# Two attention layers on one core: how the softmax denominators travel, and the order of the last two units

## The chip, the core and the metric

The kernel runs on one core of a Trainium2 chip. Its engines work side by side, each through its own list of instructions, and wait for each other by semaphores: TensorE (PE, with its weight loads shown as PEld), VectorE (DVE), ScalarE (ACT), GpSimd (POOL), and SyncE (SP), which only issues transfers. The metric is the device time of one execution in microseconds; lower is better.

## What is computed

The input is x of shape (4, 64, 32, 32): four images, 64 channels, 1024 positions. Two layers follow each other. Each does, for every image:

```
h      = group_norm(x, 32 groups)             # 2 channels x 1024 positions in a group
q,k,v  = h Wq + bq, h Wk + bk, h Wv + bv      # 1x1 convolutions, 64 -> 64
scores = q k^T / sqrt(64)                     # 1024 x 1024
attn   = softmax(scores, over the keys)
x      = x + (attn v) Wo + bo
```

The layers differ in weights and in the epsilon of the norm (1e-5, 1e-6). The second layer works on the output of the first.

## The kernel before, in words

**Units.** A unit is one image in one layer. There are UNITS = 8, in the order of the images of layer 0, then of layer 1; LAST = 7. Unit u reads `xs` slot u and writes slot u + 4. Channels lie on partitions, twice: partitions 0 to 63 hold positions 0 to 511, partitions 64 to 127 hold 512 to 1023.

**Inside a unit.** The scores are built transposed, keys on partitions, queries along the row, in eight tiles t of 128 keys by 1024 queries. ScalarE takes the exponential of each tile into `probs[t]` (L448). `values` (L843 to 853) multiplies each with `vals` and sums into `ps_attn`. The query's maximum is subtracted as an extra row `q_row` in the scores (L837, L838). It comes from a pass over partial scores made a unit ahead: `partial_max` on PE (L778, L779), eight reductions `part` on VectorE (L583), `join` (L606), a transpose `turn_max` on PE (L792), a copy `stage_max` on ScalarE (L436), and two transfers `place_rows` on SP (L246).

**The denominators.** The eight tiles of `probs` are added elementwise into `prob_sum`: `first_add` on VectorE adds tiles 0 and 1 (L613), then POOL adds tiles 2 to 7 (`add`, L322), each 128x1024. `denominators` on PE sums over the 128 partitions with eight matmuls of 128 columns against `parity`, a 0/1 pattern of two interleaved column sets; the result, 128x128, lies in `ps_misc`: quarter q of the partitions holds queries 256 q to 256 q + 255, even rows the first 128 and odd rows the second. `reciprocal` (L621) on VectorE makes `block_rden`, and eight transfers `spread_rden` bring it to `rden` (128x512), the layout of `attn`: six on SP (L256) and two on ScalarE's queue (L464); for unit 0 and unit 6 all eight on SP. `finish` on POOL (L328, L331) then multiplies `attn` by `rden` and adds x.

**Order.** In pass w of the main loop PE makes the scores of unit w and, between them, the maxima of unit w + 1; then `denominators(w - 1)`, `values(w, 0..5)`, `turn_max(w + 1)`, `project(w + 2)`, `values(w, 6)`, `project_v(w + 2)`, `values(w, 7)`. On VectorE a pass is: the eight parts with `first_add(w)` behind the third, `join`, the statistics of unit w + 2, `reciprocal(w - 1)`, then `affine`, `low_front` and `low_back` of unit w + 2. Between statistics and `affine` POOL takes the root of the variance (`root`, L303). On ScalarE: eight exps, `apply_norm(w + 2)` (L379), the two spreads, `stage_max(w + 1)`, then the copies of the projection. On SP: `place_rows(w + 1)`, the spreads of unit w - 1, four transfers that make `cross` for unit w + 2 (L229 to L238), and a store. On POOL: the adds of unit w, with `root(w + 2)` behind tile 4 and `finish(w - 1)` behind tile 5. Everything after `affine(w + 2)` on the way to `project(w + 2)` therefore waits for the root. An exp of unit w + 1 into `probs[t]` waits until tile t of unit w is added.

**The tail.** For unit 6 POOL adds only tiles 2 to 5; VectorE adds 6 and 7 to each other (`pair_tail`) and then to the sum (`add_tail`, L642). For unit 7 POOL adds tile 2 and VectorE tiles 3 to 6 (`add_late`, L651); tile 7 goes straight into the sums on PE (`denominators_last`). Units 5 and 6 are finished on VectorE (`finish_tail`, L657, L660). Unit 7's reciprocals are spread by PE (`spread_last`, L906), not by transfers.

## Time and profile before

| | us |
|---|---|
| median of three runs | 213.41 |
| lowest and highest | 212.4, 216.33 |
| the profiled execution, its own time | 212.74 |
| its span, first to last instruction | 210.9 |

| engine | busy us | share of the span | instructions |
|---|---|---|---|
| PE | 181.2 | 86% | 1295 |
| DVE | 134.3 | 64% | 200 |
| POOL | 126.0 | 60% | 79 |
| ACT | 103.1 | 49% | 137 |

The mean granted clock of TensorE was 0.95 of its full 2.4 GHz. All durations come from the profiled execution, so a sum made of them is to be set beside 212.74 or 210.9 first, and only then beside the median. Busy shares are averages over stages that have different limits; what an engine waits for is read from the timeline and the waits.

### The profile page before, as it was taken

The numbers are of one execution on the slowest core, as the hardware profiler recorded it, in microseconds if no ns is written. First come the engines' busy times: TensorE is split into PE (matmuls) and PEld (weight loads), VectorE is DVE, ScalarE is ACT, GpSimd is POOL, SyncE is SP. The second block draws the span as 40 slices with busy tenths as digits, with TensorE's granted clock in tenths as the row PEclk, the third lists the DMA queues.
The fourth block names the chain that finished last, engine by engine and source line by source line (L and its number), as shares of the span: only waits on it lengthen the run. The fifth ranks groups of instructions, "written<-read, shape, count | busy, mean of one in ns | idle before, by whom it ended". The sixth has DMA issues, their size and how long they took to land.

```text
span 210.9 us, 3456 instructions
## 1 busy us (share of the span) xinstructions
PE 181.2 (86%) x1295; PEld 100.2 (47%) x1295; DVE 134.3 (64%) x200; ACT 103.1 (49%) x137; POOL 126.0 (60%) x79
## 2 busy tenths in 40 slices
PE   7797999999997786998987994999949989995473
PEld 4444753674365421675245731576315653672332
DVE  3799894699387821499639870399605993065443
ACT  4485773684566405296077512576035850690001
POOL 3443198848508995299934999079970999603000
PEclk9999999999999996799999999699979999999679
DMA  6453000400014000320014100150001500110111
GB/s 166 144 112 79 0 0 5 100 2 3 1 48 102 5 0 13 82 55 3 0 26 99 29 0 6 34 115 2 0 16 39 149 3 12 32 56 0 40 63 50
DMA packets 8896, 8.90 MB, mean 42 GB/s; under 512 B 1656, under 2 KB 5936, under 8 KB 8880
## 3 DMA queue, kind: packets, MB, share of 16 engines
q1 hardware_dynamic: 7648, 7.90, 15.3%
q10 hardware_dynamic: 1232, 0.79, 1.3%
q8 instruction: 10, 0.16, 0.3%
q14 instruction: 6, 0.05, 0.1%
HBM read 1.58 MB, written 1.05 MB: 12 GB/s over the span
## 4 chain that ended last, share of the span: by engine, by line
POOL 41%; issue 22%; PE 15%; DVE 12%; SPq 4%; DMA 3%; POOLq 1%; ACT 0%; DVEq 0%; ACTq 0%
POOL prob_sum L322 34%; PE ps_both L853 6%; DVE part_max L583 5%; SPq L256 4%; POOL xs L331 3%; POOL attn L328 3%; DMA rden<-block_rden 2%; DMA xs<-x_dram 1%; POOLq L52 1%; DVE prob_sum L613 1%; PE ps_scores L821 1%; PE ps_max L778 1%; PE ps_scores L837 1%; DVE block_rden L621 1%; PE ps_scores L823 1%
## 5 line engine op out<-in xcount | busy, mean ns | idle before, releaser
L322 POOL TENSOR_TENSOR prob_sum<-prob_sum,probs 128x1024 f32<-128x1024 f32 x41 | 100.5, 2457 | 20.7 <-DVE prob_sum L613 17.6
L448 ACT ACTIVATE probs<-ps_scores 128x1024 f32<-128x1024 f32 x62 | 63.0, 1026 | 21.9 <-PE ps_scores L838 12.7
L853 PE MATMUL ps_both<-probs,vals 128*64 128x512 f32 x224 | 55.0, 625 | 0.0
L583 DVE TENSOR_REDUCE part_max<-ps_max 128x2 f32<-128x1024 f32 x32 | 39.1, 1221 | 11.4 <-PE ps_max L779 11.3
L853 PEld LDWEIGHTS ps_both<-probs,vals 128*64 128x64 f32 x224 | 15.1, 142 | 28.2 <-issue 26.7
L328 POOL TENSOR_TENSOR attn<-attn,rden 128x512 f32<-128x512 f32 x5 | 7.1, 1419 | 34.1 <-DMA rden<-block_rden 34.1
L583 DVE TENSOR_REDUCE part_max<-ps_both 128x2 f32<-128x1024 f32 x21 | 25.6, 1220 | 2.3 <-PE ps_both L779 2.3
L837 PE MATMUL ps_scores<-q_row,ones_r 64*128 64x512 f32 x62 | 24.5, 395 | 0.5 <-ACT q_row L430 0.5
L838 PE MATMUL ps_scores<-q_row,ones_r 64*128 64x512 f32 x62 | 24.5, 396 | 0.0
L379 ACT ACTIVATE h<-xs,shift,gain 128x512 f32<-128x512 f32 x7 | 5.7, 811 | 34.6 <-DVE shift L550 34.6
L757 PE MATMUL ps_scores<-h,layer 64*128 64x512 f32 x16 | 10.9, 764 | 10.1 <-ACT h L379 9.7
L566 DVE SCALAR_TENSOR_TENSOR front<-ps_scores,layer,front 128x512 fp32r<-128x512 f32 x6 | 4.5, 751 | 20.1 <-ACT front L390 20.1
L583 DVE TENSOR_REDUCE part_max<-ps_scores 128x2 f32<-128x1024 f32 x11 | 13.4, 1219 | 0.9 <-PE ps_scores L779 0.9
L613 DVE TENSOR_TENSOR prob_sum<-probs 128x1024 f32<-128x1024 f32 x8 | 13.4, 1670 | 0.0
L837 PEld LDWEIGHTS ps_scores<-q_row,ones_r 64*128 64x128 f32 x62 | 11.4, 184 | 3.4 <-issue 0.7
L821 PE MATMUL ps_scores<-front,back 64*128 64x512 f32 x31 | 12.9, 415 | 0.0
L822 PE MATMUL ps_scores<-back,cross 64*128 64x512 f32 x31 | 12.8, 415 | 0.0
L821 PE MATMUL ps_scores<-front,cross 64*128 64x512 f32 x31 | 12.3, 398 | 0.0
L822 PE MATMUL ps_scores<-back,front 64*128 64x512 f32 x31 | 12.3, 398 | 0.0
L826 PE MATMUL ps_scores<-back,cross 64*128 64x512 f32 x31 | 12.1, 391 | 0.0
L824 PE MATMUL ps_scores<-back,front 64*128 64x512 f32 x31 | 12.1, 391 | 0.0
L825 PE MATMUL ps_scores<-front,back 64*128 64x512 f32 x31 | 12.1, 391 | 0.0
(161 smaller groups left out, 411.5 us busy)
## 6 DMA issues: line engine op xcount, KB each, us to landing
cross<-front SPq DMA_DIRECT2D x16, 128.0 KB, 2.3
cross<-back SPq DMA_DIRECT2D x16, 128.0 KB, 2.3
rden<-block_rden SPq DMA_DIRECT2D x46, 32.0 KB, 1.9
xs<-x_dram SPq DMA_DIRECT2D x4, 256.0 KB, 4.4
out_dram<-xs SPq DMA_DIRECT2D x3, 256.0 KB, 2.0
rden<-block_rden ACTq DMA_DIRECT2D x10, 32.0 KB, 1.9
q_row<-max_rows SPq DMA_DIRECT2D x14, 2.0 KB
layer<-layers_dram SPq DMA_DIRECT2D x1, 194.5 KB, 2.7
```

The costliest lines, as they stand in the source:

```text
L322: pool.tensor_tensor(total[:, :], total[:, :], probs[t][:, :], ALU.add).then_inc(added, 1)
L328: pool.tensor_tensor(a[:, :], a[:, :], rden[:, :], ALU.mult).then_inc(normed, 1)
L448: act.activation(probs[t][:, :], scores_buffer(u, t)[:, :], ACT.Exp, scale=SCALE).then_inc(exp_done, 1)
L583: dve.tensor_reduce(part_max[u % 2][:, at:at + 2 * JS + 1:2 * JS], ps[:, :].rearrange("p (g n) -> p g n", g=2), AX.X, ALU.max, negate=True ...
L613: dve.tensor_tensor(prob_sum[u % 2][:, :], probs[0][:, :], probs[1][:, :], ALU.add).then_inc(first_added, 1)
L821: pe.matmul(left, key_top[top, hi], front_u[top, HI], start=True, stop=False)
L822: pe.matmul(right, key_low[low, hi], back_u[low, HI], start=True, stop=False)
L824: pe.matmul(right, key_low[low, hi], back_u[low, LO], start=False, stop=False)
L825: pe.matmul(left, key_top[top, lo], front_u[top, HI], start=False, stop=False)
L837: pe.matmul(left, ones_r[top, :], row[top, :], start=False, stop=True)
L838: pe.matmul(right, ones_r[low, :], row[low, :], start=False, stop=True).then_inc(scores_mm, 1)
L853: mm = pe.matmul(ps_attn[half * C:(half + 1) * C, :], v, probs[t][:, cols], start=(t == 0), stop=(t == TILES - 1))
```

## The change

- The denominators of units 0 to 6 are summed by four matmuls of 256 columns against ones, and so stand repeated on all 32 rows of a quarter. `reciprocal` for these units works on 128x256 (`quarter_rden`). Unit 7 keeps the old form.
- Spreading takes four transfers of 64 rows by 256 columns, all on SP, instead of eight of 64 rows by 128. The two on ScalarE's queue go. In passes 1 to 6 SP issues them ahead of `place_rows`.
- VectorE does `reciprocal(w - 1)` ahead of the statistics of unit w + 2 instead of behind them.
- POOL takes `root(w + 2)` behind tile 5 instead of 4, and `finish(w - 1)` behind tile 6 instead of 5.
- On PE `turn_max(w + 1)` stands behind `values(w, 4)`; `values(w, 5)` and `values(w, 6)` stand ahead of `project(w + 2)`, and the wait for `max_staged` is in every pass. In pass 6 `denominators(6)` follows `values(6, 7)`, ahead of the scores of unit 7.
- The tail: POOL adds nothing of unit 7, VectorE adds tiles 2 to 6. On VectorE the order becomes `pair_tail(6)`, `add_tail(6)`, `reciprocal(6)`, `finish_tail(5)`, `first_add(7)`, five late adds, `finish_tail(6)`, `reciprocal(7)`.

```diff
--- before.py
+++ after.py
...
     POOL_ADDS = TILES - 2
-    TAIL_ADDS = (4, 1)
+    TAIL_ADDS = (4, 0)
     HEAD_MAX = [0, 1, 2, JS, JS + 1, JS + 2, 3, JS + 3]
...
         block_rden = sb("block_rden", [P, P])
+        quarter_rden = sb("quarter_rden", [P, HALF // 2])
         rden = sb("rden", [P, HALF])
...
 
-        def rden_of(i):
-            rows = block_rden[QUARTER * (i // 2) + i % 2:QUARTER * (i // 2 + 1):2, :]
-            return rows.unsqueeze(1).broadcast_to([QUARTER // 2, 2 * C // QUARTER, P])
+        def rden_of(q):
+            return quarter_rden[quarter(q), :].unsqueeze(1).broadcast_to([QUARTER, C // QUARTER, HALF // 2])
 
...
                     sp.wait_ge(normed, u)
-                for i in range(TILES if u in (0, LAST - 1) else TILES - 2):
-                    n, j = divmod(i, JS)
-                    sp.dma_start(rden[n * C:(n + 1) * C, j * P:(j + 1) * P], rden_of(i)).then_inc(rden_in, 16)
+                for q in range(4):
+                    n, k = divmod(q, 2)
+                    sp.dma_start(rden[n * C:(n + 1) * C, k * HALF // 2:(k + 1) * HALF // 2], rden_of(q)).then_inc(rden_in, 16)
 
...
             for w in range(UNITS):
+                if 0 < w < LAST:
+                    spread_rden(w - 1)
                 if w + 1 < UNITS:
                     place_rows(w + 1)
-                if w:
+                if w == LAST:
                     spread_rden(w - 1)
...
                 a = attn[u % 2]
-                pool.wait_ge(rden_in, 128 * (u + 1))
+                pool.wait_ge(rden_in, 64 * (u + 1))
                 pool.wait_ge(attn_copied, u + 1)
...
                     add(w, t)
-                    if t == 4 and w + 2 < UNITS:
+                    if t == 5 and w + 2 < UNITS:
                         root(w + 2)
-                    if t == 5 and 0 < w < LAST - 1:
+                    if t == 6 and 0 < w < LAST - 1:
                         finish(w - 1)
...
                 act.activation(attn[u % 2][:, :], ps_attn[:, :], ACT.Copy).then_inc(attn_copied, 1)
-
-            def spread_rden(u):
-                act.wait_ge(rden_done, u + 1)
-                act.wait_ge(normed, u)
-                for i in range(TILES - 2, TILES):
-                    n, j = divmod(i, JS)
-                    act.dma_start(rden[n * C:(n + 1) * C, j * P:(j + 1) * P], rden_of(i)).then_inc(rden_in, 16)
 
...
                     apply_norm(w + 2)
-                if 1 < w < LAST:
-                    spread_rden(w - 1)
                 if w < LAST:
...
             def reciprocal(u):
-                sums = ps_misc[:, 0:P] if u < LAST - 1 else ps_max[:, HALF:HALF + P]
                 dve.wait_ge(den_mm, u + 1)
                 if u:
-                    dve.wait_ge(rden_in, 128 * u)
-                dve.reciprocal(block_rden[:, :], sums).then_inc(rden_done, 1)
+                    dve.wait_ge(rden_in, 64 * u)
+                if u < LAST:
+                    dve.reciprocal(quarter_rden[:, :], ps_misc[:, 0:HALF // 2]).then_inc(rden_done, 1)
+                else:
+                    dve.reciprocal(block_rden[:, :], ps_max[:, HALF:HALF + P]).then_inc(rden_done, 1)
 
...
                 dve.wait_ge(exp_done, TILES * LAST + t + 1)
-                if t == 3:
-                    dve.wait_ge(added, added_count(LAST, 2))
+                if t == 2:
+                    dve.wait_ge(first_added, UNITS)
                 else:
-                    dve.wait_ge(late_added, t - 3)
+                    dve.wait_ge(late_added, t - 2)
                 dve.tensor_tensor(total[:, :], total[:, :], probs[t][:, :], ALU.add).then_inc(late_added, 1)
...
                 a, n = attn[u % 2], u - LAST + 3
-                dve.wait_ge(rden_in, 128 * (u + 1))
+                dve.wait_ge(rden_in, 64 * (u + 1))
                 dve.wait_ge(attn_copied, u + 1)
...
                 join(w + 1, neg_max[:, :])
+                if w:
+                    reciprocal(w - 1)
                 if prep:
...
                     join_stats(w + 2)
-                if w:
-                    reciprocal(w - 1)
                 if prep:
...
             pair_tail(LAST - 1)
+            add_tail(LAST - 1)
+            reciprocal(LAST - 1)
             finish_tail(LAST - 2)
-            add_tail(LAST - 1)
             first_add(LAST)
-            add_late(3)
-            add_late(4)
-            reciprocal(LAST - 1)
-            add_late(5)
-            add_late(6)
+            for t in range(2, TILES - 1):
+                add_late(t)
             finish_tail(LAST - 1)
...
             def denominators(u):
-                if u == 0:
-                    pe.wait_ge(parity_set, 2)
                 if u == LAST - 1:
...
                     pe.wait_ge(added, POOL_ADDS * (u + 1))
-                if u == LAST - 1:
-                    pe.wait_ge(exp_done, TILES * LAST + 6)
-                    sums = ps_max[:, HALF:HALF + P]
-                else:
-                    sums = ps_misc[:, 0:P]
-                block_sums(sums, prob_sum[u % 2], True, True).then_inc(den_mm, 1)
+                for q in range(4):
+                    mm = pe.matmul(ps_misc[quarter(q), 0:HALF // 2], ones[:, 0:QUARTER],
+                                   prob_sum[u % 2][:, q * HALF // 2:(q + 1) * HALF // 2], start=True, stop=True)
+                mm.then_inc(den_mm, 1)
 
...
             def denominators_last():
-                pe.wait_ge(rden_done, LAST)
-                pe.wait_ge(late_added, TILES - 4)
+                pe.wait_ge(parity_set, 2)
+                pe.wait_ge(late_added, TILES - 3)
                 block_sums(ps_max[:, HALF:HALF + P], prob_sum[LAST % 2], True, False)
...
                 values(w, 4)
-                values(w, 5)
                 if w:
...
                 turn_max(w + 1)
+                values(w, 5)
+                values(w, 6)
                 if prep:
                     project(w + 2)
-                values(w, 6)
+                pe.wait_ge(max_staged, w + 2)
                 if prep:
-                    pe.wait_ge(max_staged, w + 2)
                     project_v(w + 2)
                 values(w, 7)
+                if w == LAST - 1:
+                    denominators(w)
 
...
                 scores(LAST, t)
-            pe.wait_ge(max_staged, UNITS)
+            pe.wait_ge(rden_done, LAST)
             values(LAST, 0)
             values(LAST, 1)
-            denominators(LAST - 1)
             values(LAST, 2)
...
```

## Rows read from the trace of the kernel before

**Rows 1.** The page, part 4: chain that ended last, shares of the span.

```profile
POOL 41%; issue 22%; PE 15%; DVE 12%; SPq 4%; DMA 3%; POOLq 1%; ACT 0%; DVEq 0%; ACTq 0%
```

**Rows 2.** Stages: from:to, length, busy (instructions) of each engine, PE clock, DMA share, GB/s.

```profile
39.63:59.43 19.80, 19.80 (x152) 10.73 (x151) 14.87 (x23) 12.36 (x15) 11.91 (x6) 1.00 0.10 23
59.43:88.00 28.57, 23.30 (x151) 12.47 (x149) 15.24 (x23) 12.25 (x15) 17.79 (x9) 0.88 0.15 36
...
161.31:180.44 19.13, 18.23 (x131) 9.63 (x129) 13.87 (x12) 9.07 (x10) 16.11 (x7) 1.00 0.21 52
180.44:210.90 30.46, 20.62 (x194) 13.52 (x192) 13.21 (x16) 8.67 (x10) 4.78 (x3) 0.88 0.14 42
```

**Rows 3.** Waits of POOL, whole span: instruction, releaser, total us, times, longest.

```profile
POOL attn L328 <- DMA rden<-block_rden: 34.1, 5, 8.1
```

**Rows 4.** Timeline of unit 3: start us, us, engine, line, operation, count, [idle before, releaser].

```profile
102.28 0.95 DVE L621 RECIPROCAL block_rden<-ps_both 128x128 f32<-128x128 f32 x1
...
104.19 0.55 POOL L303 TENSOR_TENSOR rstd<-var_eps,minus_half 128x1 f32<-128x1 f32 x1
...
105.20 0.81 ACT L379 ACTIVATE h<-xs,shift,gain 128x512 f32<-128x512 f32 x1 [5.71 <-DVE shift L550]
105.27 1.20 ACTq L464 DMA_DIRECT2D rden<-block_rden  x2
106.57 0.27 ACT L436 ACTIVATE max_rows<-ps_both 8x128 fp32r<-8x128 f32 x1 [0.55 <-issue]
...
106.86 1.35 SPq L246 DMA_DIRECT2D q_row<-max_rows  x2
108.31 3.81 SPq L256 DMA_DIRECT2D rden<-block_rden  x6
...
113.43 1.29 POOL L328 TENSOR_TENSOR attn<-attn,rden 128x512 f32<-128x512 f32 x1 [6.37 <-DMA rden<-block_rden]
```

**Rows 5.** Timeline of PE, unit 1 and the start of unit 2.

```profile
39.56 0.50 PE L778 MATMUL ps_max<-back,front 64*128 64x512 f32 x1
...
50.07 5.37 PE L853 MATMUL ps_both<-probs,vals 128*64 128x512 f32 x24
55.37 0.27 PE L792 MATMUL ps_both<-const_sb,neg_max 128*8 128x128 f32 x1
55.58 0.69 PE L757 MATMUL ps_scores<-h,layer 64*128 64x512 f32 x1
...
59.38 0.49 PE L778 MATMUL ps_max<-back,front 64*128 64x512 f32 x1
```

**Rows 6.** Timeline of PE, the last unit.

```profile
188.31 1.95 PE L860 MATMUL ps_both<-probs,vals 128*64 128x256 f32 x16
190.19 0.65 PE L868 MATMUL ps_max<-prob_sum,parity 128*32 128x128 f32 x16
...
204.93 1.09 PE L906 MATMUL ps_max<-block_rden,const_sb 128*64 128x128 f32 x16 [1.54 <-DVE block_rden L621]
```

**Rows 7.** Timeline of DVE, unit 1.

```profile
43.56 1.22 DVE L613 TENSOR_TENSOR prob_sum<-probs 128x1024 f32<-128x1024 f32 x1
...
50.96 0.68 DVE L516 BATCH_NORM_STATS2 stats<-xs 128x6 f32<-128x512 f32 x1
```

**Rows 8.** Timeline of POOL, units 0 and 1.

```profile
25.68 7.44 POOL L322 TENSOR_TENSOR prob_sum<-prob_sum,probs 128x1024 f32<-128x1024 f32 x3 [7.78 <-DVE prob_sum L613]
...
44.92 7.44 POOL L322 TENSOR_TENSOR prob_sum<-prob_sum,probs 128x1024 f32<-128x1024 f32 x3 [3.42 <-DVE prob_sum L613]
52.85 0.55 POOL L303 TENSOR_TENSOR rstd<-var_eps,minus_half 128x1 f32<-128x1 f32 x1 [0.49 <-DVE var_eps L537]
```

**Rows 9.** Timeline of ACT and DVE, the last unit.

```profile
181.98 1.95 ACT L448 ACTIVATE probs<-ps_scores 128x1024 f32<-128x1024 f32 x2 [0.82 <-PE ps_scores L838]
...
191.86 2.55 DVE L651 TENSOR_TENSOR prob_sum<-prob_sum,probs 128x1024 f32<-128x1024 f32 x2 [2.61 <-POOL prob_sum L322]
```

**Rows 10.** Line L613, the first add: durations of all eight.

```profile
L613 DVE TENSOR_TENSOR prob_sum<-probs x8: 1215/1444/2635, 24.3 to 188.0; 128x1024 f32<-128x1024 f32 x8
```

## The prediction

> **What bounds the kernel now.** I read the chain that ended last first. POOL holds 41% of it and "issue", time with no visible wait, 22% [rows 1]; no engine is the bound all through. The table by stages then shows that the units differ. A unit here is one pass of the main loop, from its first `ps_max` matmul to the next one's. Unit 1 took 19.80 us with PE busy for all of it; unit 2 took 28.57 with 23.30 busy, and the last unit, all tail, 30.46 with 20.62 busy, both at a lower granted clock [rows 2]. Units 2 to 5 together go from 59.43 to 161.31, a mean of 25.5. Unit 1 is the one in which POOL ends its adds without a `finish` that delays the next ones, so it shows what a unit costs when nothing holds it. The waits name what holds the others: POOL stood 34.1 us, in five pieces, in front of `finish`, until `rden` had landed [rows 3].
>
> The timeline of unit 3 shows the loop [rows 4]. POOL takes the root at 104.19; ScalarE applies the norm at 105.20, then issues its two spreads (105.27, 1.20 us), and only then stages the maxima (106.57); SP places the rows (106.86, 1.35 us), issues six spreads (108.31, 3.81 us), and POOL's multiply starts at 113.43. But the reciprocal that feeds those spreads started at 102.28 and was over, after 0.95 us, at 103.23. From there to the multiply 10.2 us pass, of which the data needs only its own issue and landing (the last issue starts at 108.31 + 5 x 0.64 = 111.5; to 113.43 it is 1.9 us). Behind the multiply stand the second half of `finish` and five adds, and then the next root. So the loop is root, norm, staging, rows, spreads, `finish`, five adds, root. It closes on itself, and its length is what each unit pays.
>
> **The steady unit after the change.** I build it from unit 1, all times from the unit's start s (39.56 in unit 1).
>
> 1. PE. Values start at s + 10.5; six tiles take 5.30 us (50.07 to the transpose at 55.37), 0.88 each, the transpose 0.2 [rows 5]. Now seven tiles and the transpose stand ahead of the projection: ready at 10.5 + 7 x 0.88 + 0.2 = s + 16.9. From the projection to the next unit 3.80 us passed (55.58 to 59.38) with one tile among them that now lies ahead: 2.92 remain.
> 2. Denominators. Four matmuls of 256 columns replace eight of 128, onto the same four 32-row quarters. The trace has no such form. The same columns in the same quarters took 0.65 us (16 records at 190.19); one after the other the new ones would take 1.9, since 16 records of 256 columns took 1.88 (188.31 to 190.19) with two column halves at once [rows 6]. I take 0.65, the row nearest in placement. At 1.9 PE comes to the projection at s + 18.2.
> 3. Reciprocal. It grows from 128 to 256 columns: 0.95 us if width were free, 1.9 if it is twice the present one [rows 4]. I take 1.75, nearly proportional. It now starts behind the join, at s + 11.4, where the statistics stood (50.96) [rows 7], and ends at s + 13.15. The statistics, and the root after them, now queue behind its wait for the denominators; these are done at s + 10.6. Statistics to root took 1.9 us (50.96 to 52.85) [rows 7, 8], so the variance is there at s + 15.05, at worst 15.2.
> 4. Root. POOL starts its adds at s + 5.36 (44.92); three took 7.44 us, so four with their gaps take 10.0: the root starts at s + 15.4 [rows 8]. It is one add later than before, but the variance would hold it nearly as long. Root to the end of the norm took 1.82 us (104.19 to 106.01) [rows 4]: the projection starts at s + 17.2, 0.3 us after PE is ready. Hence the period: 17.2 + 2.9 = 20.1 us.
> 5. Spreads. SP issues four instead of six, and ScalarE none, which takes 1.20 us out between norm and staging. At 0.64 us each from s + 13.2 the last starts at s + 15.15 and lands 1.9 later, s + 17.1. POOL reaches `finish` at 15.4 + 0.55 + 2.5 = s + 18.4: the wait is gone with 1.3 to spare. On SP the rows, the swaps and a store queue behind the spreads. Staging ends at s + 17.5, the rows land by about s + 20 and are wanted 1 us into the next unit, s + 21. The swaps follow the high halves, at s + 19 and later, when all spreads are long issued.
> 6. POOL after `finish`: 2.7 us (two halves of 1.3) and one add, 2.5, end at 18.4 + 5.2 = s + 23.6, 3.5 us into the next unit. VectorE's first add starts at 4.0 (43.56 less 39.56) [rows 7]; half a microsecond to spare.
>
> Unit 0 has no `finish`, but its root moves behind one more add: three adds end at 33.12 [rows 8], the fourth at 35.65, the projection starts at 37.45 and unit 1 at 40.4, 0.8 us later than now. Five units of 20.1 give unit 6 at 140.9, against 161.31 [rows 2]: 20.4 us earlier.
>
> **The tail.** Unit 6 has no projection: values at 10.5, eight tiles 7.04 and the transpose 0.2, then the denominators, 0.65: 18.5, so unit 7 starts at 159.4. PE's new wait for the staging costs nothing, since one small ScalarE copy stands against two tiles of values. The denominators wait for VectorE's `add_tail`: POOL's four adds end near s + 15.4, or 16.4 after a collision with `pair_tail`, and 1.2 more gives 17.6, before PE's 17.8. The scores of unit 7 stand behind this wait, so what is lost here counts in full.
>
> Now the last unit waits for POOL's `add(7, 2)`, for two late adds, a reciprocal and two more; then eight spreads follow. After the change VectorE does the reciprocal and `finish_tail(5)` in the first 3.3 us, and the first add at 3.5, when the second exp is done (181.98 + 1.95 less 180.44); five late adds of 1.25 (2.55 for two) follow [rows 2, 9]: done at 3.5 + 1.2 + 6.2 = 10.9. PE does the scores in 7.87 (180.44 to 188.31) and four tiles in 3.76, and is at the last sums at 11.6: they no longer wait. Two sets of sums take 1.3, two tiles 1.88: the last spread on PE starts at 14.8. `finish_tail(6)`, two operations of half the first add's width, 1.4 with gaps, fits between 10.9 and the last reciprocal at 12.9. From PE's spread (204.93) to the end of the span, 210.9, 5.97 us passed [rows 6]. So the last unit takes 20.8 instead of 30.46, and the span ends at 180.2.
>
> The profiled execution took 212.74 for its span of 210.9: 1.84 around it, so 182.0. The median of the runs, 213.41, lies 0.67 over it: 182.7.
>
> **A rule that speaks against it.** The first add took 1.22 us with POOL at rest and up to 2.64 beside POOL's adds [rows 7, 10]. The Trainium skill, "SBUF — State Buffer", section "SBUF: two separate sides", says that a VectorE operation with two SBUF inputs and a GpSimd operation that reads SBUF take a shared port pair for the whole instruction, so that one blocks the other. By that rule the cover of step 6 is a cliff and not a slope; the trace's spread agrees with it, and the sum by it is rival A's if the cover fails, and mine if it holds.
>
> **Rivals.**
>
> A. POOL comes later than step 6 says, and its add meets VectorE's first. Price: 2.64 - 1.22 = 1.4 us a unit, and everything behind it moves. Six units: 8.4, so 191. For: only 0.5 us spare. Against: every term up to there is from undisturbed rows. The dearer denominators of step 2 (1.0 a unit, 6 us, 189) end near it. 0.19.
>
> B. The change doesn't open the loop: something else, such as spreads of twice the bytes that land much later, holds `finish` as long as the rows do now. It takes the 1.3 us of step 5 and 5 more. Then only the tail gains, 9.7 less 0.8 for unit 0: 204.5. Against: the spreads' 1.9 us show no queue ahead. 0.07.
>
> C. As B, and the denominators of unit 6 stop PE by 5 us or more, since POOL's adds are then late: 210 to 214, no change. 0.04.
>
> D. Slower. The rows now stand behind the spreads on SP, and these wait for the multiply of the unit before (`normed`). If that is late, the rows are late, PE stops at the first scores, exps and adds follow, and so does the next multiply. From the multiply to landed rows it takes four issues, two row issues and a landing, about 5 us. The whole comes out above today's from a unit of 26.3 (30.7 us over five units above 20.1), with rows landing at s + 27.3 and the multiply at s + 22; it is forecast at s - 0.4, so this decides only when it is a whole unit late. At 27.3 a unit the time would be about 219. 0.04.
>
> **How the numbers follow.** The forecast has 0.66 and its own range is 178.5 to 186: below, the root is no bound, PE alone sets 19.8 (1.5 us less) and the tail's sums are quicker; above, 0.7 us a unit. To reach 8 in 10 the range takes in A: 178.5 to 192. What a measurement can tell from no change is about 2%, 209.1 to 217.7. Faster by more: 0.66 + 0.19 + 0.07 = 0.92; within: 0.04; slower: 0.04.
>
> **What would show it.** Right: units 1 to 5 at about 20 us each, granted clock 1.00 in all of them; POOL's wait before its multiply near nothing, its idle time now before the first of its adds; reciprocals of about 1.75 us; the last unit 20 to 21 us with no PE gap before its sums. Wrong: first adds of 2 us or more (A), long waits for `rden` at the multiply (B), PE idle after unit 6's values (C), PE waiting for `q_row` (D).

## The result, and the profile after

| | before | after |
|---|---|---|
| median, us | 212.91 (212.19 to 216.33, four runs) | 181.54 (180.99 to 182.0, four runs) |
| profiled execution, its own time | 212.74 | 181.74 |
| its span | 210.9 | 179.9 |
| mean granted clock | 0.95 | 1.00 |

The ratio is 0.8535, with a 95% interval of 0.849 to 0.8581. Ratios, here and below, leave out executions that lie more than 1.5% above the fastest of their kernel, as 216.33 does. The forecast was 182.7.

Three lines of the page of after: busy time by engine, the chain that ended last, and the spreads (transfers, KB each, us from issue to landing):

```profile
PE 172.9 (96%) x1239; PEld 93.7 (52%) x1239; DVE 139.8 (78%) x201; ACT 102.5 (57%) x137; POOL 118.7 (66%) x78
...
PE 64%; POOL 17%; DVE 13%; issue 2%; ACT 2%; POOLq 0%; DVEq 0%
...
rden<-quarter_rden SPq DMA_DIRECT2D x28, 64.0 KB, 2.1
```

POOL's 41% and the 22% of "issue" [rows 1] are now 17% and 2%, and PE, the engine with the most work, is busy for 96% of the span.

The table by stages of after, from one unit's start to the next (columns as in [rows 2]); units 2, 4 and 5 look like the first two lines (20.06, 20.07, 20.06 us):

```profile
41.00:61.07 20.07, 20.02 (x144) 10.44 (x143) 15.81 (x24) 12.17 (x16) 14.78 (x9) 1.00 0.18 41
...
81.13:101.23 20.10, 20.05 (x145) 10.46 (x143) 15.84 (x24) 12.19 (x16) 17.25 (x10) 1.00 0.17 40
...
141.36:159.85 18.49, 18.49 (x131) 9.53 (x129) 17.21 (x14) 9.58 (x12) 12.52 (x6) 1.00 0.23 58
159.85:179.90 20.05, 16.82 (x180) 12.08 (x176) 14.23 (x16) 8.22 (x10) 0.00 (x0) 1.00 0.17 54
```

The 31.0 us of the span divide by [rows 2]: unit 6 starts at 141.36 instead of 161.31 (19.95), takes 18.49 instead of 19.13 (0.64), and the last unit takes 20.05 instead of 30.46 (10.41).

All of POOL's waits of after that come to 6 us or more (columns as in [rows 3]):

```profile
POOL prob_sum L324 <- DVE prob_sum L606: 24.3, 7, 7.8
POOL rstd L305 <- DVE var_eps L530: 6.0, 2, 3.2
```

The 34.1 us in front of the multiply are gone altogether. POOL now idles before the first of its adds, where nobody waits for it.

The timeline of after, unit 3, which starts at s = 81.13 (columns as in [rows 4]):

```profile
86.49 9.95 POOL L324 TENSOR_TENSOR prob_sum<-prob_sum,probs 128x1024 f32<-128x1024 f32 x4 [2.34 <-DVE prob_sum L606]
...
92.55 1.75 DVE L614 RECIPROCAL quarter_rden<-ps_both 128x256 f32<-128x256 f32 x1
...
94.32 2.53 SPq L256 DMA_DIRECT2D rden<-quarter_rden  x4
...
95.77 0.21 DVE L530 TENSOR_SCALAR var_eps<-moments,eps 128x1 f32<-128x1 f32 x1
...
96.40 0.55 POOL L305 TENSOR_TENSOR rstd<-var_eps,minus_half 128x1 f32<-128x1 f32 x1
...
97.42 0.81 ACT L381 ACTIVATE h<-xs,shift,gain 128x512 f32<-128x512 f32 x1 [5.65 <-DVE shift L543]
98.41 1.30 SPq L246 DMA_DIRECT2D q_row<-max_rows  x2
99.22 1.28 POOL L330 TENSOR_TENSOR attn<-attn,rden 128x512 f32<-128x512 f32 x1
...
101.82 2.41 POOL L324 TENSOR_TENSOR prob_sum<-prob_sum,probs 128x1024 f32<-128x1024 f32 x1
```

Before, the spreads were issued behind the rows (108.31 behind 106.86), and these behind root and norm [rows 4]. Now SP issues the spreads when the reciprocal ends, 2 us before the root, and places the rows 4 us later. The multiply at 99.22 follows the add in front of it without idle time. POOL's last add ends 3.0 us into the next unit (101.82 + 2.41 less 101.23).

### The profile page after: what moved, and what is told of

Its sections match the earlier page's. It is cut to its first block, busy times and chain, and to the rows that moved or that the text cites. A ratio compares the mean times of both kernels' runs of the same rounds, so it can differ in the third digit from the quotient of the medians.

```text
span 179.9 us, 3311 instructions
## 1 busy us (share of the span) xinstructions
PE 172.9 (96%) x1239; PEld 93.7 (52%) x1239; DVE 139.8 (78%) x201; ACT 102.5 (57%) x137; POOL 118.7 (66%) x78
## 4 chain that ended last, share of the span: by engine, by line
PE 64%; POOL 17%; DVE 13%; issue 2%; ACT 2%; POOLq 0%; DVEq 0%
PE ps_both L846 17%; POOL prob_sum L324 16%; DVE part_max L576 10%; PE ps_scores L814 5%; PE ps_scores L830 5%; PE ps_scores L750 5%; PE ps_scores L816 5%; PE ps_scores L818 4%; PE ps_both L758 4%; PE ps_both L853 4%; PE ps_max L771 3%; PE ps_scores L722 3%; DVE prob_sum L606 2%; PE ps_both L871 2%; PE ps_both L771 1%
## 5 line engine op out<-in xcount | busy, mean ns | idle before, releaser
L324 POOL TENSOR_TENSOR prob_sum<-prob_sum,probs 128x1024 f32<-128x1024 f32 x40 | 95.1, 2377 | 27.5 <-DVE prob_sum L606 24.3
L846 PE MATMUL ps_both<-probs,vals 128*64 128x512 f32 x224 | 52.2, 598 | 0.0
L846 PEld LDWEIGHTS ps_both<-probs,vals 128*64 128x64 f32 x224 | 14.6, 136 | 24.1 <-issue 23.0
L559 DVE SCALAR_TENSOR_TENSOR front<-ps_scores,layer,front 128x512 fp32r<-128x512 f32 x6 | 4.5, 751 | 17.2 <-ACT front L392 17.2
L614 DVE RECIPROCAL quarter_rden<-ps_both 128x256 f32<-128x256 f32 x7 | 12.3, 1751 | 1.0 <-PE ps_both L871 1.0
L814 PE MATMUL ps_scores<-front,cross 64*128 64x512 f32 x31 | 12.3, 396 | 0.0
L816 PE MATMUL ps_scores<-front,cross 64*128 64x512 f32 x31 | 12.1, 391 | 0.0
L818 PE MATMUL ps_scores<-front,cross 64*128 64x512 f32 x31 | 12.1, 391 | 0.0
```

Source lines behind the costliest of these rows:

```text
L324: pool.tensor_tensor(total[:, :], total[:, :], probs[t][:, :], ALU.add).then_inc(added, 1)
L614: dve.reciprocal(quarter_rden[:, :], ps_misc[:, 0:HALF // 2]).then_inc(rden_done, 1)
L814: pe.matmul(left, key_top[top, hi], front_u[top, HI], start=True, stop=False)
L816: pe.matmul(left, key_top[top, hi], front_u[top, LO], start=False, stop=False)
L818: pe.matmul(left, key_top[top, lo], front_u[top, HI], start=False, stop=False)
L846: mm = pe.matmul(ps_attn[half * C:(half + 1) * C, :], v, probs[t][:, cols], start=(t == 0), stop=(t == TILES - 1))
```

## The experiments

Each is the changed kernel with one thing undone, or the kernel before with one part of the change, unless it says otherwise. Ratios are to the kernel before, run beside it on the same chip. Rows and lengths of units come from one execution of each kernel.

### The place of the spreads on SP

The first kernel is the changed one with the rows issued first again:

```diff
-                if 0 < w < LAST:
-                    spread_rden(w - 1)
                 if w + 1 < UNITS:
                     place_rows(w + 1)
-                if w == LAST:
+                if w:
                     spread_rden(w - 1)
```

> The changed kernel with one thing undone: on SP the rows are placed first and the four spreads follow, as before the change. Theory (the loop through the rows was the cost, and the place of the spreads is what opened it): rows are staged 17.3 us into a unit, SP issues them to 18.8 and the spreads to 21.3, they land at 23.2, so POOL waits 4.9 us at its multiply; multiply to root is then 2.6 + 2.4 + 10.0 and root to multiply 7.9, a period of 23.0 instead of 20.1. Five units of it: 196 us. Rival (the gain comes from four transfers instead of eight and from ScalarE issuing none): 2 us at most over the changed kernel, 183.5.

Measured: 199.64 us (199.25 to 203.05), ratio 0.9323 (0.9237 to 0.9409). The trace is of the execution that took 203.05, the longest of five. Three views of it: POOL's wait, two stages, the timeline of SP and POOL in the unit that starts at 83.77.

```profile
POOL attn L328 <- DMA rden<-quarter_rden: 23.5, 5, 4.7
```

```profile
83.77:109.79 26.02, 22.70 (x143) 11.57 (x141) 16.26 (x24) 12.35 (x16) 18.13 (x9) 0.87 0.18 43
109.79:130.86 21.07, 20.32 (x143) 10.45 (x142) 16.17 (x23) 12.15 (x15) 17.29 (x9) 1.00 0.11 24
```

```profile
104.31 1.34 SPq L246 DMA_DIRECT2D q_row<-max_rows  x2
105.75 2.54 SPq L256 DMA_DIRECT2D rden<-quarter_rden  x4
...
109.89 1.29 POOL L328 TENSOR_TENSOR attn<-attn,rden 128x512 f32<-128x512 f32 x1 [4.73 <-DMA rden<-quarter_rden]
```

The loop is back: rows, spreads, multiply, adds, root, with everything else of the change in place. POOL's wait of 4.7 us is near the expected 4.9, but the time came out 3.6 us above the expectation. VectorE and PE, in the same unit and in the last one:

```profile
104.18 1.22 PE L748 MATMUL ps_scores<-h,layer 64*128 64x512 f32 x1 [3.32 <-ACT h L379]
...
179.91 1.76 DVE L612 RECIPROCAL quarter_rden<-ps_both 128x256 f32<-128x256 f32 x1 [4.63 <-DMA rden<-quarter_rden]
...
190.87 0.64 PE L859 MATMUL ps_max<-prob_sum,parity 128*32 128x128 f32 x16 [3.72 <-DVE prob_sum L644]
```

Two things were not in the expectation. A late norm costs twice: PE stood 3.3 us before the projection, and the work from there to the next unit then took 5.61 us (104.18 to 109.79) at a granted clock of 0.50, where the changed kernel does it in 2.95 at 1.00. In the next unit, where PE idled for 0.75 us (21.07 less 20.32), the clock is 1.00 and the unit 5 us shorter. And the last unit took 25.40 us (175.90 to 201.3) instead of 20.05: the spreads of unit 5 are behind the rows too, VectorE's reciprocal waits for them, its adds end late, and PE stands before the last sums. In this trace the last unit is 5.35 us of the excess over the changed kernel, and units 1 to 5 are 16.1, where 14.5 was expected. The four shorter executions have no trace; their mean granted clocks, 0.957 to 0.974, show that PE was slowed in them too.

The second is the other direction, the kernel before with only this order changed on SP:

```diff
+                if 0 < w < LAST:
+                    spread_rden(w - 1)
                 if w + 1 < UNITS:
                     place_rows(w + 1)
-                if w:
+                if w == LAST:
                     spread_rden(w - 1)
```

> The kernel before with one thing of the change: SP issues its six spreads ahead of the rows. ScalarE still issues two behind the norm, and the tail, the reciprocals, the root and PE's order are as before. Theory: the loop is open. The last spread is now ScalarE's second, landing about 4.2 us behind the root; POOL is there 3.1 us behind it, waits 1 us, and its last two adds run 1.4 us into the next first add of VectorE, so units of 20 to 21 us instead of 25.5: four units, 193 to 196 us. Rival (every part is needed, since two spreads still wait for the norm): 208 us or more.

Measured: 195.29 us (195.07 to 195.42), ratio 0.9126 (0.9058 to 0.9193). Units 2 to 5 took 22.18, 21.15, 21.02 and 21.17 us. Its wait of POOL before the multiply, and its first adds (durations ns min/median/max):

```profile
POOL attn L330 <- DMA rden<-block_rden: 14.3, 5, 4.5
```

```profile
L615 DVE TENSOR_TENSOR prob_sum<-probs x8: 1214/1840/3124, 24.8 to 167.8; 128x1024 f32<-128x1024 f32 x8
```

One swapped pair of lines brings some 18.6 us, 0.0874 of the 213 before. What is left in this kernel is a wait of about 3 us a unit, and late adds of POOL that meet the first add. The time is as expected, the wait is not: it was put at 1 us, with ScalarE's second spread as the last to land. In unit 3 (from 82.10) the spreads on SP start only 15.7 us into the unit, at 97.80, and their six issues take 3.79 us. ScalarE's two are issued from 98.08 to 99.35, before SP's last, so POOL waits for SP's.

### How much the form of the spreads and the place of the reciprocal carry

Two kernels. In the first, `stats_first`, VectorE does the statistics ahead of the reciprocal again:

```diff
-                if w:
-                    reciprocal(w - 1)
                 if prep:
...
                     join_stats(w + 2)
+                if w:
+                    reciprocal(w - 1)
```

> The changed kernel with VectorE's order undone: the statistics first, then the reciprocal. Theory (this edit only buys cover): the reciprocal ends 15.0 us into the unit instead of 13.2, the spreads land at 19.1, POOL's multiply is 1.0 us later than its 18.1, and its last add ends 4.1 us into the next unit, just where the first add starts. The root stays bound by POOL's adds. 181.5 to 183.5 us, with 0.8 to 1.1 us of POOL waiting for rden in each unit. Rival (the place of the reciprocal is what opened the loop): 189 us or more.

The second, `eight_spreads`, keeps the old denominators, `block_rden` and eight transfers of 128 columns, all on SP. The transfers:

```diff
-                for q in range(4):
-                    n, k = divmod(q, 2)
-                    sp.dma_start(rden[n * C:(n + 1) * C, k * HALF // 2:(k + 1) * HALF // 2], rden_of(q)).then_inc(rden_in, 16)
+                for i in range(TILES):
+                    n, j = divmod(i, JS)
+                    sp.dma_start(rden[n * C:(n + 1) * C, j * P:(j + 1) * P], rden_of(i)).then_inc(rden_in, 16)
```

> The changed kernel with the old form of denominators (eight matmuls against the 0/1 pattern, reciprocal of 128 columns, eight transfers), all eight on SP and ahead of the rows. Theory (the number of transfers is not what gained): the reciprocal ends at 12.4 us instead of 13.2, eight issues take 5.1, the last lands at 18.8, POOL's multiply is 0.7 us later, inside the 0.9 it has before the next first add. 181.5 to 182.5 us. Rival (four transfers fewer a unit are worth their 2.5 us of issue): 189 us or more.

Measured: 181.57 us (181.16 to 181.96), ratio 0.8494 (0.8439 to 0.8548), and 182.37 us (181.98 to 183.18), ratio 0.8543 (0.8494 to 0.8591). By their ratios neither can be told from the changed kernel. In both POOL waits again before the multiply; the timeline of POOL in the first:

```profile
100.53 1.29 POOL L330 TENSOR_TENSOR attn<-attn,rden 128x512 f32<-128x512 f32 x1 [1.07 <-DMA rden<-quarter_rden]
```

Five such waits come to 5.5 us in the first and 4.7 in the second, and the units stay at 20.07 to 20.11. POOL had 1.0 us between its last add and VectorE's first (3.0 against 4.0 us into the unit); a delay of that size is absorbed. The longest first adds, where POOL was latest, took 1.41 and 1.57 us instead of 1.22. So in the loop these parts of the change buy cover only.

The second kernel has one wait more. Eight issues keep SP for 5.06 us (from 153.86), the rows of unit 7 are placed behind them, at 158.97, and PE has to stand for them in the last unit, which takes 20.75 us instead of 20.05:

```profile
161.38 0.50 PE L830 MATMUL ps_scores<-q_row,ones_r 64*128 64x512 f32 x1 [0.48 <-DMA q_row<-max_rows]
```

### The order on PE

In `project_early` the changed kernel has the old order on PE again:

```diff
                 values(w, 4)
+                values(w, 5)
                 if w:
                     pe.wait_ge(rden_done, w)
                 turn_max(w + 1)
-                values(w, 5)
-                values(w, 6)
                 if prep:
                     project(w + 2)
+                values(w, 6)
```

> The changed kernel with PE's order undone: the transpose behind values 5 and the projection right behind it, values 6 after it. Theory (root to projection sets the period now, and the moved values fill PE's time until the norm is done): PE comes to the projection at 16.1 us, stands until 17.15, and has 3.8 us to go instead of 2.9: 0.85 us a unit, six units, 186.6 us. Rival (POOL or VectorE is the bound, so PE's order is free): 181.5 to 182.5.

Measured: 186.57 us (186.08 to 187.0), ratio 0.8719 (0.865 to 0.8788), as expected. PE in unit 3, which starts at 83.77:

```profile
100.92 0.69 PE L750 MATMUL ps_scores<-h,layer 64*128 64x512 f32 x1 [1.06 <-ACT h L381]
```

With one tile less in front, PE stands 1.06 us before the projection, and each unit takes 20.95 instead of 20.07. The granted clock stays 1.00 here. The move of one tile over the projection is worth 0.88 us a unit, 5 us in all.

### The order on POOL, and rival A's collision

In `pool_early` the changed kernel has the old order on POOL again:

```diff
-                    if t == 5 and w + 2 < UNITS:
+                    if t == 4 and w + 2 < UNITS:
                         root(w + 2)
-                    if t == 6 and 0 < w < LAST - 1:
+                    if t == 5 and 0 < w < LAST - 1:
                         finish(w - 1)
```

> The changed kernel with POOL's order undone: root behind tile 4, finish behind tile 5. Theory (rival A of the prediction as a price: POOL's adds must be over before VectorE's first add starts, 4.0 us into a unit): finish then starts at about 18.1 us as now, but two adds follow it instead of one and end 5.5 us into the next unit. The first add takes 2.5 to 3.2 us instead of 1.2, the maxima, the reciprocal and the statistics behind it are 1.5 us late, and the root, now waiting for the variance, comes at 16.5: units of 21.3 instead of 20.1, 187.5 us. Rival (the same work in another order, and the root 0.3 us earlier): 180 to 182 us, first adds at 1.2.

Measured: 183.76 us (183.7 to 184.52), ratio 0.8611 (0.8565 to 0.8657), between the two expected numbers. `finish` is now followed by two adds instead of one, and the second meets VectorE's first add. The timeline around the start of the unit at 80.20:

```profile
80.73 4.93 POOL L324 TENSOR_TENSOR prob_sum<-prob_sum,probs 128x1024 f32<-128x1024 f32 x2
...
84.20 2.54 DVE L606 TENSOR_TENSOR prob_sum<-probs 128x1024 f32<-128x1024 f32 x1
...
96.03 0.55 POOL L305 TENSOR_TENSOR rstd<-var_eps,minus_half 128x1 f32<-128x1 f32 x1 [1.72 <-DVE var_eps L530]
```

The mechanism is rival A's, and its first adds take 2.5 us in the median. VectorE's add starts at 84.20, POOL's adds end at 80.73 + 4.93 = 85.66, and 85.66 plus an undisturbed add of 1.22 gives 86.88; it ended at 86.74. VectorE thus held still until POOL's add was over. The section of the Trainium skill behind rival A ("SBUF — State Buffer", "SBUF: two separate sides") says that "the other fully blocks", and the row agrees. The price is less than forecast: a unit takes 20.74 instead of 20.07, 0.67 us and not 1.4. The five reductions behind the add run without gaps, 1.13 us from start to start, and make up 0.4 of 1.3; the variance starts 0.9 us later (s + 15.54 against s + 14.64), and the root, which in the changed kernel has to wait for the fourth add anyway, 0.6 later. In unit 0, where nothing collides, the early root gains 0.7 us (20.78 against 21.48). Units 2 to 5 lose 0.56, 0.64, 0.68 and 0.7 us, and unit 6 0.9 (142.45 to 161.83, 19.38 against 18.49); units 0 and 1 gain 0.7 and 0.1. That leaves 2.7, where the medians are 2.2 apart. In unit 6 `add_tail` ended at 161.21, just as PE came to the denominators (161.26).

### The tail, alone and with the order on SP

The tail is that of the changed kernel in the kernel before: its core is

```diff
-    TAIL_ADDS = (4, 1)
+    TAIL_ADDS = (4, 0)
...
                 values(w, 7)
+                if w == LAST - 1:
+                    denominators(w)
```

with VectorE's new order and the new place of PE's wait for `rden_done`.

> The kernel before with the new tail alone: denominators of unit 6 at the end of its pass, VectorE's new order, POOL adding nothing of unit 7; still eight spreads of the old form. Theory: the tail is worth 9.7 us only if POOL is on time in unit 6. With the loop closed its adds of unit 6 end at 183.0, VectorE's add 1.2 us later, and PE, free at 180.4, stands about 4 us ahead of the scores of unit 7: 9.7 - 4.5 = 5.2 us gained, 208 us, with an idle time of PE of some 4 us before the denominators. Rival (tail and loop add up, each by itself): 203.7 us.

Measured: 209.48 us (208.84 to 210.18), ratio 0.9791 (0.9712 to 0.987). VectorE and PE at the end of unit 6, and the stage behind it:

```profile
183.67 1.23 DVE L642 TENSOR_TENSOR prob_sum<-prob_sum,late_sum 128x1024 f32<-128x1024 f32 x1 [7.31 <-POOL prob_sum L322]
...
184.95 0.65 PE L866 MATMUL ps_both<-prob_sum,parity 128*32 128x128 f32 x16 [3.82 <-DVE prob_sum L642]
```

```profile
184.95:189.00 4.05, 4.05 (x36) 3.14 (x38) 2.20 (x3) 1.34 (x2) 0.00 (x0) 0.67 0.06 15
```

This is what rival C described: POOL's adds are late, `add_tail` with them, and PE stands 3.82 us before the denominators, with all scores of unit 7 behind them. Then it runs at a mean granted clock of 0.67. Alone the tail brings some 4.5 us (2.8 to 6.1 by the interval), where the last unit of the changed kernel gained 10.4.

> The kernel before with two things of the change: SP issues its spreads ahead of the rows, and the new tail. Theory (the tail is worth its full gain once the loop no longer delays POOL): unit 6 starts at 145.4 as with the order alone, takes 18.5 to 19.5, and the last unit 20.6: a span of 185, 187 us, that is 8 us less than the order alone, where the tail by itself gained 5 to the kernel before. Rival (the tail is worth the same with and without the loop): 190 us.

This is the kernel before with the two lines on SP swapped and the same tail. Measured: 189.84 us (188.13 to 190.47), ratio 0.8888 (0.8837 to 0.8939): the number of the rival. Its stages around the denominators of unit 6:

```profile
163.90:166.50 2.60, 0.55 (x16) 0.38 (x16) 1.23 (x1) 0.60 (x1) 0.67 (x1) 1.00 0.00 1
166.50:171.00 4.50, 4.50 (x30) 3.58 (x28) 2.19 (x3) 1.77 (x2) 0.00 (x0) 0.62 0.18 66
```

PE stood 2.08 us before the denominators, and over the next 4.50 us the clock was 0.62, part of that stretch at 1.2 GHz. The work from these sums to the first values of unit 7 took 9.74 us (165.95 to 175.69) and takes 8.16 in the changed kernel (159.28 to 167.44), so the stall of 2.1 us cost about 3.7. The fourth execution, at 188.13 us, had a mean clock of 0.999 where the others had 0.988: in it the slow stretch seems not to have come.

In the changed kernel `add_tail` is in time. No single one of the other parts is needed for that: with PE's old order, with the statistics first, with eight spreads and, by a hair, with POOL's old order PE did not wait for it. Which of them together bring it about was not tested.

### A better kernel: whose engine applies the norm

After the change PE still waits a little for the norm (97.42 + 0.81 = 98.23, projection at 98.28). Three kernels try to shorten this, beside the changed kernel once more.

> The changed kernel itself, beside the next two on the same chip: 181.5 us.

Measured: 181.09 us (180.89 to 182.01), ratio 0.8502 (0.8465 to 0.8538); units of 20.05 to 20.09, unit 0 21.45.

The first, `split_norm`, lets VectorE apply the second half of the norm while ScalarE does the first:

```diff
+            def apply_norm_half(u):
...
+                dve.tensor_scalar(h[:, HALF // 2:HALF], xs[:, at + HALF // 2:at + HALF], gain[:, u:u + 1],
+                                  shift[:, u:u + 1], ALU.mult, ALU.add).then_inc(half_h, 1)
```

> The changed kernel with the norm of units 2 to 7 applied in halves: ScalarE takes the first 256 columns, VectorE, idle at that time, the other 256. Theory (PE waits 0.2 us in each unit for the norm, and nothing else holds it): ScalarE's 0.81 us becomes 0.60, the projection starts 0.2 us earlier, and PE alone sets the unit, 19.85 us instead of 20.08: 1.2 us less, 180.3 us. Rival (another wait, such as the high halves or VectorE's parts, is just behind): no change, 181.5.

Measured: 188.64 us (188.39 to 190.82, and one execution at 333.14 that nothing here explains), ratio 0.886 (0.8812 to 0.8909). Both numbers missed by 7 us or more. The new operation, by its line (durations ns) and in the timeline of the unit behind 65.14:

```profile
L558 DVE TENSOR_SCALAR h<-xs,gain,shift x6: 1997/2001/2008, 37.2 to 145.4; 128x256 f32<-128x256 f32 x6
```

```profile
80.91 2.36 POOL L324 TENSOR_TENSOR prob_sum<-prob_sum,probs 128x1024 f32<-128x1024 f32 x1
...
81.41 2.01 DVE L558 TENSOR_SCALAR h<-xs,gain,shift 128x256 f32<-128x256 f32 x1
```

The same form took 0.41 us once in the head of this kernel, with POOL at rest. Beside POOL's add it takes 2.0, all six times, until about the end of that add. Units grew to 21.33 us, 1.26 more, and unit 0 to 24.31, where PE stood 1.81 us and its clock fell to 0.93 in the mean. The trace is of the execution at 190.82; the ones at 188.4 to 188.9 had a mean clock of 0.998 or 0.999 instead of 0.991, so that fall is not in all of them.

The second adds POOL's root behind tile 4 in unit 0:

```diff
-                    if t == 5 and w + 2 < UNITS:
+                    if t == (5 if w else 4) and w + 2 < UNITS:
```

> As split_norm, and in unit 0 POOL takes the root behind tile 4 again, since no finish follows there. Theory: unit 0 gets back what the later root cost it, 0.7 us of the 0.85 between 20.63 and 21.48: 179.6 us. Rival: unit 0 is bound by PE's new order of values and projection and not by the root, 180.3 us.

Measured: 186.69 us (186.55 to 187.44), ratio 0.8762 (0.8728 to 0.8796). Unit 0 took 20.78 us, so this part holds; the split still costs in the others, and the time missed both numbers.

The third keeps that root and leaves the norm on ScalarE, in two halves of 256 columns, and PE projects each half as it comes:

```diff
+                    for c in range(2):
+                        cols = slice(c * HALF // 2, (c + 1) * HALF // 2)
...
+                    for c in range(2):
+                        pe.wait_ge(*((half_h, u), (h_ready, u + 1))[c])
+                        pe.matmul(projected(u)[:, a:b], p[0:C, 0:P], h[0:C, a:b], start=True, stop=True)
```

> The changed kernel with two edits. In unit 0 POOL takes the root behind tile 4. In units 2 to 7 ScalarE applies the norm in two halves of 256 columns and PE projects the first half while the second is made; VectorE is left out of it, since its 256-column operation took 2.00 us beside POOL's add. Theory: unit 0 falls by 0.7 us, from 21.45 to 20.8. The halves take about 0.55 each, so the second is done at 1.1 instead of 0.8, but only half of the projection, 0.5 us, follows it: 0.2 us less a unit, 19.85 instead of 20.08, if the high halves and VectorE's parts allow it. 179.2 us, against 181.1 for the changed kernel. Rival (only the root of unit 0 gains, and a unit stays at 20.08 or gets longer by the extra loads on PE): 180.4 us or more.

Measured: 180.31 us (179.89 to 181.0), ratio 0.8439 (0.8403 to 0.8474). ScalarE and PE in the unit behind 60.10:

```profile
76.36 1.09 ACT L388 ACTIVATE h<-xs,shift,gain 128x256 f32<-128x256 f32 x2 [5.62 <-DVE shift L550]
...
77.14 0.48 PE L756 MATMUL ps_scores<-h,layer 64*128 64x256 f32 x1
```

PE starts on the first half before the second is there (76.36 + 1.09 = 77.45) and doesn't wait. Two halves cost ScalarE 1.09 us instead of 0.81. Units took 19.97 to 19.99 us and unit 0 20.78: 0.7 us from unit 0, but only 0.1 from each other unit, where 0.2 was expected, so the time lies by the rival's number. This is the fastest kernel of the study. Its interval and that of the repeat just overlap, so the time alone is thin evidence; the lengths of the units carry it.

## Why the prediction was right

**Step 1, PE.** Right. In unit 3 (s = 81.13) the projection started at s + 17.15 (98.28 less 81.13) where 17.2 was forecast; 2.95 us remained. PE was ready 0.2 us earlier: in `project_early`, with one tile of 0.88 less in front of the projection, it stood 1.06. Its order is worth 5 us by its own experiment.

**Steps 2 and 3, denominators and reciprocal.** The four matmuls of 256 columns took 0.64 us (the row at 159.28 below), so the choice by placement, not by column count, was right. The reciprocal took 1.75 us in all seven, as chosen between 0.95 and 1.9. It ended at s + 13.17 (94.30), the variance was there at s + 14.85 where 15.05 was forecast.

**Step 4, root.** Forecast s + 15.4, measured s + 15.27. The period of 20.1 stands at 20.06 to 20.10.

**Step 5, spreads.** The last issue was forecast at s + 15.15 and lies near it (94.32 + 3 x 0.63 = 96.2, s + 15.1). The landing takes 2.1 us instead of 1.9, and POOL reached the multiply at s + 18.1 instead of 18.4: 0.9 us to spare by these, not 1.3. `stats_first` shows what is behind it: 1.07 us of wait at no cost to the unit.

**Step 6, rival A.** POOL's last add ended 3.0 us into the unit, not 3.5, so the cover is 1.0 us and not 0.5. The term of the price was mis-sized: 0.67 us a unit instead of 1.4, since the reductions behind the first add have slack. With it rival A would have given 182.7 + 6 x 0.67 = 186.7 and not 191, and the range could have ended lower. The end of the cover was called a cliff. It is none for the time: the first add waits out only what is left of POOL's add, so it took 1.41 us in the one unit of `stats_first` where it started 0.3 us before POOL's end, and 2.54 in `pool_early`, 1.46 us before it.

**Unit 0.** 21.48 us, at 0.8 us more than now as forecast. That this loss had a simple cure, the root behind tile 4 in this unit alone, the prediction did not see.

**The tail.** The timeline of after, DVE and PE, from the end of unit 6 on (the last unit starts at 159.85):

```profile
154.47 3.26 DVE L630 TENSOR_TENSOR late_sum<-probs 128x1024 f32<-128x1024 f32 x1
157.76 1.23 DVE L637 TENSOR_TENSOR prob_sum<-prob_sum,late_sum 128x1024 f32<-128x1024 f32 x1
159.28 0.64 PE L871 MATMUL ps_both<-prob_sum,ones 128*32 128x256 f32 x8
...
159.99 1.76 DVE L614 RECIPROCAL quarter_rden<-ps_both 128x256 f32<-128x256 f32 x1 [1.00 <-PE ps_both L871]
...
164.42 6.54 DVE L646 TENSOR_TENSOR prob_sum<-prob_sum,probs 128x1024 f32<-128x1024 f32 x5
...
171.11 0.64 PE L861 MATMUL ps_max<-prob_sum,parity 128*32 128x128 f32 x16
...
173.90 1.04 PE L895 MATMUL ps_max<-block_rden,const_sb 128*64 128x128 f32 x16
```

`add_tail` ended at 158.99, s + 17.63, where 17.6 was forecast, 0.3 us before PE wanted it. Unit 6 took 18.49 of 18.5. In the last unit the late adds ended at 170.96, 11.1 into it (forecast 10.9), and PE's sums started 0.15 behind them, where the forecast had them free of a wait at 11.6: PE came earlier than thought, its scores having taken 7.59 and not 7.87, four tiles 3.67 and not 3.76. The two sets of sums took 1.01 and not 1.3, two tiles 1.78 and not 1.88. The last spread on PE thus started at 14.05 instead of 14.8, and 6.0 us follow, where 5.97 had been read. All of the last unit's 0.75 us below the forecast is here.

**From the span to the time.** The 1.84 us around the span came again. That the median would lie 0.67 over the profiled execution did not; it lay 0.2 below. With the last unit's 0.75 and unit 6's start 0.46 late (141.36 against 140.9; unit 0 itself began 0.57 later than before, at 19.5, which the repeat, at 18.96, doesn't show), the sum 182.7 - 0.75 + 0.46 - 0.87 = 181.54 closes. Of the 1.2 us that the forecast is too high, 0.87 is how executions scatter; that the rest nearly cancels is luck.

**Rivals.** B, late landing of the wider spreads, did not come: they land in 2.1 us. What came back when the rows went first (199.64) is the old loop. C's stop of PE came in the kernel before with the tail alone, where POOL stays late (3.82 us). Of D the first half did appear: with the rows behind the spreads on SP, PE waited for `q_row` 0.74, 0.43 and 0.19 us in the kernel before with the new order on SP, 0.73 once with the tail added, and 0.48 in `eight_spreads`, all of which issue six or eight spreads there. In the changed kernel, with four, it never did. D's runaway through a late multiply wasn't tested.

## What to carry to other kernels

Where a queue issues in order, ask of each transfer which semaphore the one ahead of it waits for: data that was ready 10 us early stood behind rows that needed the root, and the swap of two lines brought 18.6 of 31 us. Then ask how late a late arrival may be: delays of 1 us that fell into a cover of 1.0 cost the loop nothing, so fewer and wider transfers weren't what made this kernel fast. And ask what the order puts off in its turn: the rows now stand behind the spreads, and with eight of these PE waited for them once. Before an operation is put on another engine, look at what its neighbour does in that moment, and price a stall of PE with what its clock does afterwards.

## What the runs showed of the hardware

**VectorE beside GpSimd.** While GpSimd (POOL) adds 128x1024 out of SBUF (2.4 us each), three operations of VectorE took longer: the first add 2.54 us instead of 1.22, `pair_tail` 3.26 instead of 1.16, and, what I had not expected, an operation with a single SBUF input, `tensor_scalar` on 128x256, 2.00 instead of 0.41. The reductions and the reciprocal from PSUM kept their 1.2 and 1.75 us beside the same adds. The Trainium skill, "SBUF — State Buffer", section "Who interferes with whom", names `tensor_scalar` among the operations that can take the shared pair; the row agrees. It also says that "issue order, not op shape, decides who blocks", and `pair_tail` shows both sides: in the changed kernel it took 3.26 us and POOL's four adds 9.92; with the statistics first it began 0.2 us earlier against POOL's adds (7.53 us behind their start, not 7.75), took 1.16, and POOL's adds took 10.90. `add_tail` ended at 158.99 in one and 159.40 in the other.

**The clock after a pause of PE.** Pauses of 2.08 and 3.82 us were followed by 4.5 and 4.05 us at a mean granted clock of 0.62 and 0.67, and one of 3.32 us by 5.61 us at 0.50, which is 1.2 GHz. One of 1.81 us stands in a unit with a mean of 0.93. Pauses of 1.06 us, one in each unit, and of 1.25 to 1.29 us in the units of `split_norm` left it at 1.00. What such a pause costs is its length and then the slow stretch: 2.1 and 1.6 us, 3.8 and 1.6 (184.95 to 194.68 is 9.73 us against 8.16), 3.3 and 2.7. The slow stretch need not follow in every execution of a kernel, as the mean clocks of 0.999 beside 0.988 and 0.998 beside 0.991 show.

**Small prices.** A reciprocal from PSUM goes by its width: 0.95 us for 128 columns, 1.75 for 256. Four matmuls of 256 columns on the four 32-row quarters take what eight of 128 do, 0.64 us. A 64 KB spread lands 2.1 us after its issue, a 32 KB one 1.9 (medians), and SP takes 0.63 us to issue either (four in 2.53 us, eight in 5.06).
